# A graph kernel: TensorE gathers 12 groups of edges instead of 7, in a PSUM bank of its own

## What is computed

```python
msgs = z[edge_dst] @ Wd + z[edge_src] @ Ws + edge_weight[:, None] * ww[None, :] + bm
agg = jax.ops.segment_max(msgs, edge_dst, num_segments=n)
hidden = jax.nn.relu(z @ W1a + agg @ W1b + b1);  x1 = layernorm(x + hidden @ W2 + b2)
# then two SAGE convolutions on x1: mean over the edges, two linear maps, relu between
x = layernorm(x1 + conv2(relu(conv1(x1))))
```

## Time and profile before

| | us |
|---|---|
| median of 3 runs | 1136.53 (1135.17 to 1138.17) |
| profiled execution | 1136.4, its span 1134.6 |
| busy: TensorE, VectorE, GpSimd, ScalarE | 997.1, 894.9, 757.0, 500.8 |
| mean granted clock of TensorE | 0.958 |

### The profile page before, as it was taken

The page is one execution under the profiler, slowest core; times in us unless marked ns, Lnnn a source line. Parts: engine busy times, 40 slices in busy tenths (PEclk is TensorE's granted clock), DMA queues, the critical chain, the costliest instruction groups (busy, mean ns, idle before and its releaser), DMA issues.

```text
span 1134.6 us, 23462 instructions
## 1 busy us (share of the span) xinstructions
PE 997.1 (88%) x6407; PEld 735.8 (65%) x6449; DVE 894.9 (79%) x3127; ACT 500.8 (44%) x1434; POOL 757.0 (67%) x802
## 2 busy tenths in 40 slices
PE   4689999999997999978797879886889899899997
PEld 4367767767765777756665656565556577656776
DVE  6488999999886999897777778777788788746455
ACT  3256766666542656533333323333324233312664
POOL 6657777777777777777777777777777777200332
PEclk9789999999997999989898889999999999999999
DMA  8724344344344343334434334433344354446221
GB/s 210 214 61 94 92 98 109 94 99 114 89 97 106 91 119 97 91 85 127 110 87 93 90 97 129 105 91 89 87 132 110 106 150 97 117 134 177 83 58 42
DMA packets 123128, 121.14 MB, mean 107 GB/s; under 512 B 24307, under 2 KB 106392, under 8 KB 122989
## 3 DMA queue, kind: packets, MB, share of 16 engines
q1 hardware_dynamic: 95920, 69.21, 22.7%
q0 software_dynamic: 23968, 49.13, 18.0%
q10 hardware_dynamic: 3101, 1.21, 0.4%
HBM read 105.60 MB, written 13.88 MB: 105 GB/s over the span
## 4 chain that ended last, share of the span: by engine, by line
PE 36%; POOL 30%; issue 15%; DVE 12%; DMA 3%; SPq 2%; ACT 1%; ACTq 1%; DVEq 0%
POOL area L1037 30%; PE bank L1910 7%; PE bank L1748 5%; PE bank L1685 5%; PE bank L1675 3%; PE bank L1626 3%; PE bank L1785 3%; DVE area L1225 2%; DVE area L1209 2%; PE bank L1665 2%; PE bank L1875 2%; DVE area L1208 2%; PE bank L1614 2%; PE bank L1861 1%; PE bank L1706 1%
## 5 line engine op out<-in xcount | busy, mean ns | idle before, releaser
L1037 POOL DMA_INDIRECT area<-zs_d,area x729 | 705.4, 968 | 234.8 <-issue 219.3
L863 ACT CAST adj_w<-bank 128x325 f32 x391 | 176.2, 451 | 472.5 <-PE bank L1685 415.1
L1225 DVE TENSOR_TENSOR_SCAN area<-area,bank 128x512 f32<-128x512 bf16 x196 | 249.7, 1274 | 144.1 <-PE bank L1626 126.5
L1209 DVE TENSOR_SCALAR area<-area 128x325 bf16<-128x325 f16 x782 | 249.5, 319 | 0.0
L1685 PE MATMUL bank<-area 128*128 128x104 f32 x1564 | 234.0, 294 | 0.1
L1208 DVE TENSOR_SCALAR area<-area 128x128 bf16<-128x128 f16 x782 | 212.1, 271 | 0.0
L1685 PEld LDWEIGHTS bank<-area 128*128 128x128 f32 x1564 | 204.7, 204 | 11.3 <-ACT area L869 1.9
L1675 PE MATMUL bank<-area 128*128 128x325 bf16 x782 | 157.2, 316 | 22.0 <-DVE area L1210 15.8
L1626 PE MATMUL bank<-ident,area 128*128 128x128 f32 x734 | 123.1, 291 | 45.8 <-DMA area<-zs_d,area 45.4
L1626 PEld LDWEIGHTS bank<-ident,area 128*128 128x128 f32 x734 | 78.1, 142 | 91.1 <-DMA area<-zs_d,area 57.2
L1748 PE MATMUL bank<-adj_w,area 128*128 128x512 bf16 (+5 forms) x497 | 108.5, 357 | 24.6 <-DMA area<-parts_d 8.6
(11 more groups left out here) (174 smaller groups left out, 1067.6 us busy)
## 6 DMA issues: line engine op xcount, KB each, us to landing
area<-mask_d SPq DMA_DIRECT2D x195, 128.0 KB
area<-zs_d,area POOLq DMA_INDIRECT x729
area<-zs_d SPq DMA_DIRECT2D x640, 0.5 KB
area<-parts_d SPq DMA_DIRECT2D x20, 384.0 KB, 7.6
area<-wp_d SPq DMA_DIRECT2D x195, 9.0 KB
zr_d<-area SPq DMA_DIRECT2D x24, 128.0 KB
area<-zr_d SPq DMA_DIRECT2D x6, 512.0 KB, 4.5
area<-scale_d SPq DMA_DIRECT2D x11, 256.0 KB, 4.3
```

The lines of the kernel that those rows point to most:

```text
L863: nc.scalar.copy(adj[:, :, bass.ds(at, W)], A_BANK[s % 2][:, 0:COLS].rearrange("p (h w) -> p h w", w=W))
L1037: pool.indirect_dma_start(gring[:, g % GR * 4 + s % 2 * 2 + u, :], None, x if g < RAW else zs_d[0:N, :], bass.IndirectOffsetOnAxis(ap=firs ...
L1209: nc.vector.tensor_scalar(hot_d[:, r, u, :], i_key[:, 0:COLS], key_n[:, u, s:s + 1], None, ALU.is_equal)
L1225: nc.vector.tensor_tensor_scan(S[:, g % 2, 0:n], mask[:, g % MR, 0:n], (L_BANK if g in PICKED else T_BANK[g % 2])[:, 0:n], S[:, (g + 1) % ...
```

## The change

- PICKS has 12 groups instead of 7. The first is gathered in slots 20 to 29, and each next one starts in the slot in which the one before is used, up to slot 145. A pick takes 10 or 11 slots, so a slot has two or three one-hots; before, there were 8 to 11 slots, from 7 to 92, with gaps at 48 and 49, 60 to 70, and 80 to 84.
- The picks add up in G_BANK, the bank that was M1. Waits between picks and pieces or degree rows go. Picks now stand in slots with pieces and degree rows.
- x transposed and roots move to M0 (for the last two tiles to G_BANK). New waits: `outputs` of a tile for the roots' copy of the tile before, x transposed for `y_sb`. `roots` and `copy_zr` come one slot sooner.
- `hidden` becomes `hidden_of` on ScalarE, same slot, one activation with bias and relu.
- The one-hots lie in blocks of 128 words, one in each of 2 or 4 rows of the adjacency matrix (SPARE = 1185); the bf16 ones in free columns of aggT, in 3 buffers instead of 4. The group's numbers are made floats in place, and their next load waits for `keyed`.

```diff
-PICKS = ((17, 7), (28, 17), (37, 28), (48, 37), (60, 50), (80, 71), (93, 85))
+PICKS = ((30, 20), (40, 30), (51, 40), (61, 51), (72, 61), (82, 72), (93, 82), (103, 93), (114, 103), (124, 114), (135, 124),
+         (145, 135))
+RAWS = 3
-SPARE = 801
+SPARE = 1185
-        key_i = adj_w[:, spare(0, 512)].bitcast(i32)
-        key_w = adj_w[:, spare(1, 512)]
-        keys = [adj_w[:, spare(2, 256, 256 * i)].bitcast(f16) for i in range(2)]
+        def spare(row, rows):
+            return adj_w.rearrange("p (h n) -> p h n", n=ROW)[:, row:row + rows, SPARE:SPARE + P]
+        key_w = spare(0, 4)
+        key_i = key_w.bitcast(i32)
+        keys = [spare(4 + 2 * i, 2).bitcast(f16) for i in range(2)]
+        hot_b = [aggT[:, FREE + 256 * i:FREE + 256 * i + 256].bitcast(bf16) for i in range(RAWS)]
+        def x_bank(t):
+            return (M0 if t < NT - 2 else G_BANK)[:, P:2 * P]
+        def root_bank(t):
+            return M0[:, P:3 * P] if t < NT - 2 else G_BANK[:, 2 * P:4 * P]
...
                 def load_key(i):
-                        sp.wait_ge(key_float, i)
+                        sp.wait_ge(keyed, i)
...
+                def hidden_of(t):
+                    act.wait_ge(v_ps, t + 1)
+                    nc.scalar.activation(hid(t)[:, 0:k], M0[:, 0:k], ACT.Relu, bias=c0_c).then_inc(hid_sb, 1)
...
                 def make_hot(i, h):
-                    if u >= HOTS:
-                        dve.wait_ge(hot_cast, u - HOTS + 1)
+                    if u >= RAWS:
+                        dve.wait_ge(hot_cast, u - RAWS + 1)
...
                 def x_turned(t):
-                    if t >= 2:
-                        pe.wait_ge(zr_sb, t - 1)
-                    nc.tensor.transpose(M1[:, P:P + k], x_rows(t)[0:k, :], ident[0:k, 0:k]).then_inc(xr_ps, 1)
+                        pe.wait_ge(y_sb, min(t, NT - 2))
+                    if t == NT - 2:
+                        pe.wait_ge(scanned, PICKED[-1] + 1)
+                    nc.tensor.transpose(x_bank(t)[:, 0:k], x_rows(t)[0:k, :], ident[0:k, 0:k]).then_inc(xr_ps, 1)
...
                 def outputs(t):
+                        pe.wait_ge(zr_sb, min(t, NT - 2))
...
                 def half_piece(c, j, h0, h1, at):
-                        pe.wait_ge(scanned, picked_before(PIECES[c][0]) + 1)
...
                 def pick_rows(i, h):
-                        before = len([p for p in PIECES if p[0] < a])
-                        if before:
-                            pe.wait_ge(acc_sb, before)
-                        rows = len([d for d in DEGREE_SLOTS if d < a])
-                        if rows:
-                            pe.wait_ge(deg_sb, rows)
...
-                    for t in tiles(k, 12, -1):
+                    for t in tiles(k, 11):
                         roots(t)
```

More of the change, by code:

```diff
@@ L54 @@
 HOTS = 4
+RAWS = 3
 ROW = AW // 2
-SPARE = 801
+SPARE = 1185
+FREE = 2 * SPARE
 NODES = "a source node, which is below N"
@@ L229, in gnn_kernel @@
         zs_low = [z[:, :, low_at:ROW] for z in zs_r]
-        def spare(row, n, lead=0):
-            return slice(row * ROW + SPARE + lead, row * ROW + SPARE + lead + n)
-        key_i = adj_w[:, spare(0, 512)].bitcast(i32)
-        key_w = adj_w[:, spare(1, 512)]
-        keys = [adj_w[:, spare(2, 256, 256 * i)].bitcast(f16) for i in range(2)]
-        hot_b = [adj_w[:, spare(3 + i // 2, 256, 256 * (i % 2))].bitcast(bf16) for i in range(HOTS)]
-        hot_r = [nc.alloc_sbuf_tensor_at(f"hot_r{i}", [P, 512], f32r, offset=adj_at + 32 * ((ROW * (5 + i) + SPARE) // 8))[:, :]
-                 for i in range(HOTS)]
+        def spare(row, rows):
[3 more added lines that the diff above has]
+        keys = [spare(4 + 2 * i, 2).bitcast(f16) for i in range(2)]
+        hot_r = [nc.alloc_sbuf_tensor_at(f"hot_r{i}", [P, 4 * ROW], f32r, offset=adj_at + 32 * ((ROW * (8 + 4 * i) + SPARE) // 8))[:, :]
+                 .rearrange("p (h n) -> p h n", n=ROW)[:, :, 0:P] for i in range(HOTS)]
         AREA = 15776
@@ L565, in load_key @@
                     if i:
-                        sp.wait_ge(key_float, i)
-                    sp.dma_start(key_i, src[512 * g:512 * g + 512].rearrange("(o e) -> o e", o=1).broadcast_to([P, 512])).then_inc(l_key, 16)
+                        sp.wait_ge(keyed, i)
+                    row = src[512 * g:512 * g + 512].rearrange("(o a e) -> o a e", o=1, e=P)
+                    sp.dma_start(key_i, row.broadcast_to([P, 4, P])).then_inc(l_key, 16)
                 def load_sources():
@@ L885, in copy_x1T @@
                     nc.scalar.copy(zr_of(t)[:, 0, 0:size(t)], M0[:, 384:384 + size(t)]).then_inc(x1T_sb, 1)
+                def hidden_of(t):
+                    k = size(t)
+                    act.wait_ge(v_ps, t + 1)
+                    if 0 < t < NT - 1:
+                        act.wait_ge(x1_st, 32 * t)
+                        act.wait_ge(parts_sb, t)
+                        act.wait_ge(x1T_sb, t)
+                    nc.scalar.activation(hid(t)[:, 0:k], M0[:, 0:k], ACT.Relu, bias=c0_c).then_inc(hid_sb, 1)
                 def copy_zr(t):
@@ L889, in copy_zr @@
                     for a in range(2):
-                        last = nc.scalar.activation(zr_of(t)[:, a, 0:size(t)], M1[:, (2 + a) * P:(2 + a) * P + size(t)], ACT.Identity, bias=b1l_c[:, a:a + 1])
+                        last = nc.scalar.activation(zr_of(t)[:, a, 0:size(t)], root_bank(t)[:, a * P:a * P + size(t)], ACT.Identity, bias=b1l_c[:, a:a + 1])
                     last.then_inc(zr_sb, 1)
@@ L925, in usual @@
                             key_to_float(i)
-                    for t in tiles(k, 13, -1):
+                    for t in tiles(k, 12):
                         copy_zr(t)
@@ L929, in usual @@
                         copy_x1T(t)
+                    for t in tiles(k, 4):
+                        hidden_of(t)
                     for t in tiles(k, 7):
@@ L1249, in scale_from @@
                     nc.vector.reciprocal(row, row).then_inc(scale_sb, 1)
[L1251 to L1258, removed]
                 def stats(t):
@@ L1295, in key_of @@
                     dve.wait_ge(key_float, i + 1)
-                    nc.vector.tensor_scalar(keys[i % 2], key_w, float(CENTER), None, ALU.subtract).then_inc(keyed, 1)
+                    nc.vector.tensor_scalar(keys[i % 2].rearrange("p a (b e) -> p a b e", e=P), key_w.rearrange("p (a b) e -> p a b e", b=2),
+                                            float(CENTER), None, ALU.subtract).then_inc(keyed, 1)
                 def make_hot(i, h):
@@ L1300, in make_hot @@
                     dve.wait_ge(keyed, i + 1)
-                    if u >= HOTS:
-                        dve.wait_ge(hot_cast, u - HOTS + 1)
-                    nc.vector.tensor_scalar(hot_b[u % HOTS], keys[i % 2], node_c[:, h:h + 1], None, ALU.is_equal).then_inc(hot_made, 1)
+                    if u >= RAWS:
+                        dve.wait_ge(hot_cast, u - RAWS + 1)
+                    nc.vector.tensor_scalar(hot_b[u % RAWS].rearrange("p (a e) -> p a e", a=2), keys[i % 2], node_c[:, h:h + 1], None,
+                                            ALU.is_equal).then_inc(hot_made, 1)
                 for k in range(SLOTS):
@@ L1319, in usual @@
                         stats(t)
-                    for t in tiles(k, 4):
-                        hidden(t)
                     if k in DEGREE_SLOTS[:6]:
@@ L1611, in rows_T @@
                 if g in PICKED:
-                    nc.tensor.matmul(L_BANK[:, :], ww9[0:9, :], wp9[:, g % WR, 0:n], start=False, stop=True).then_inc(t_ps, 1)
+                    nc.tensor.matmul(G_BANK[:, :], ww9[0:9, :], wp9[:, g % WR, 0:n], start=False, stop=True).then_inc(t_ps, 1)
                     return
@@ L1741, in roots @@
                     for a in range(2):
-                        last = nc.tensor.matmul(M1[:, (2 + a) * P:(2 + a) * P + k], w1r[:, a * P:(a + 1) * P], zr_of(t)[:, 0, 0:k], start=True, stop=True)
+                        last = nc.tensor.matmul(root_bank(t)[:, a * P:a * P + k], w1r[:, a * P:(a + 1) * P], zr_of(t)[:, 0, 0:k], start=True, stop=True)
                     last.then_inc(zr_ps, 1)
@@ L1784, in pick_rows @@
                     for part_of in (zs_high[at], zs_low[at]):
-                        last = nc.tensor.matmul(L_BANK[:, :], part_of[0:n, h - SPLITS[at][1], :], hot_r[u % HOTS][0:n, :],
+                        last = nc.tensor.matmul(G_BANK.rearrange("p (a e) -> p a e", e=P), part_of[0:n, h - SPLITS[at][1], :], hot_r[u % HOTS][0:n],
                                                 start=h == 0 and part_of is zs_high[at], stop=False)
```

15 lines of the change are left out of this document (4 added, 11 removed).

## The result

The changed kernel takes 1152.39 us, median of 4 runs (1150.39 to 1155.16), beside 1136.3 for the one before. The ratio on record is 1.0126, 95% interval 1.0094 to 1.0157; these two medians alone give 1.0142, inside it. It is slower by 14 to 16 us, where 6.5 were forecast; the sign and the mechanism were right, the size was not. The execution that was profiled is the slowest of the four, 2.8 us above the median.

What follows compares the result with a forecast made beforehand. GpSimd's gathers bound the kernel; alone they would put group 149's gather at 719, but TensorE holds it to 747, against 740.5 before: 1136.4 + 6.5 = 1143 us, own range 1135 to 1152, with rivals 1118 to 1157.

Steps and rivals of the forecast that it cites:

- T: Slots 50 to 146: TensorE's own list of work is longer than GpSimd's, because of where the picks stand.
- the signs of being right: Expected: 709 gathers, 20 to 35 us more GpSimd waiting for TensorE, nearly all in slots 70 to 145.
- GpSimd's part: Main loop: twenty gathers fewer save 25.2 us, 125 more one-hots give back 4.7, leaving 20.5 us.
- rival D: GpSimd's gathers: each new one-hot blocks a gather for its whole length, adding 44.6 us: 1156 us; chance 0.05.
- TensorE's sum: Slots 50 to 146: slots, one-hots, pieces, degree rows and stalls sum to 485.4 us, taken as 476.4.
- the credit: Slots 50 to 146: 9 us off for picks and pieces sharing a slot, bounds 0 and 16.8.
- The three fixed stalls: Slots 66 to 70, 98 to 102, 130 to 134: reciprocal delays store, loads and first piece; 27.6, 24.0, 24.0 us.
- the landmark: First gather of group 149, past the last new pick: from 740.5 to 747.0, so +6.5 us.
- C: Half-piece slots: VectorE is late, half a microsecond in each of 25, giving 1156 us; chance 0.12.
- B: Slots 50 to 146: TensorE absorbs the picks in about 448 us; 1116 us, up to 1130; chance 0.28.
- E: VectorE: the strided one-hots run at 627 ns, 81 us more, giving about 1200 us; chance 0.05.
- The edits costed at nothing: Activation on ScalarE, earlier roots, shared bank M0, key-load wait, three raw buffers, 128-word one-hot rows: priced at 0 us.

Runs made afterwards that it cites:

- high part only: Changed kernel with only each one-hot's product with the table's high part, 300 of 600 matmuls left out: 0.9955 of the kernel before.
- thin pieces: Changed kernel, the eight pieces starting in slots 102 to 138 each keeping one matmul of twelve: 1.0080 of the kernel before, 1144.8 us.
- both reliefs: Changed kernel with only high-part products and every second one-hot a VectorE pass over 16 columns: 0.9890 of the kernel before, 1122.8 us.

## Why the prediction was right in sign and short in size

**What bounds the kernel** was read rightly. GpSimd set the pace before, TensorE and VectorE were within a few per cent of it wherever picks stood; the picks moved into slots that lacked the room, and the ring of four groups carried that back to GpSimd. T is shown from both sides: taking TensorE's work away (high part only, thin pieces) shortens slots 50 to 146 by 25.5 and 20.4 us in the traces, taking the picks out of slots 103 to 145 costs nothing, and eleven picks placed by TensorE's room are faster than the kernel before. One reading of the trace was too strong: behind the wait of 8.57 us GpSimd was held once more, 1.71 us before the gather at 70.88, and only then never again; nothing of the sum hangs on it. Of the signs of being right, the place of the waits came true (45 us of them in slots 70 to 145), their amount did not: 43 us more than before, where 20 to 35 were expected.

**GpSimd's part.** 20.5 us were put on twenty gathers; with both reliefs the trace shows 449.3 us for 448. The price of 0.038 us per one-hot held. GpSimd's gathers after the change, from 270 to 750 us and from 785 to 985, and the one-hots of the first stretch:

```profile
L1051 POOL DMA_INDIRECT area<-zs_d,area x343 | 334.4, 975 | 147.3 <-issue 97.3 <-PE bank L1631 46.1 <-PE bank L1617 4.0
...
L1051 POOL DMA_INDIRECT area<-zs_d,area x159 | 151.7, 954 | 48.5 <-issue 47.9 <-PE bank L1631 0.6
...
L1309 DVE TENSOR_SCALAR area<-adj_w,node_c 128x512 bf16<-128x512 f16 x225 | 70.3, 360 | 0.2
```

A gather is 21 ns longer where one-hots are made: 0.021 x 343 / 225 = 0.032 us per one-hot. This also settles rival D. Its 0.357 us per one-hot would have made these gathers some 230 ns longer. The Trainium skill's page SBUF — State Buffer (section "Who interferes with whom") has VectorE's two-port passes and GpSimd's descriptor writing exclude each other; here, beside two or three one-hot passes in a slot, a gather is those 21 ns longer, and no run shows in which mode the passes run or what each single meeting costs.

**TensorE's sum** was good until its last line. Group 50 opened at 271.3 for 273.5, because GpSimd began group 20 at 121.0 and not 123.0. From there the rows came to 485.4, and 487.4 were measured. The step that failed is the credit: "I take 9", for picks and pieces that share a slot. In the sum it measured nothing. Opening matmuls of groups 111 to 113, and 128 and 129:

```profile
576.12 0.38 PE L1619 MATMUL bank<-area,ww 9*128 9x512 bf16 x1
...
579.98 0.38 PE L1619 MATMUL bank<-area,ww 9*128 9x512 bf16 x1
...
585.14 0.39 PE L1619 MATMUL bank<-area,ww 9*128 9x512 bf16 x1
...
660.87 0.38 PE L1619 MATMUL bank<-area,ww 9*128 9x512 bf16 x1
...
665.80 0.39 PE L1619 MATMUL bank<-area,ww 9*128 9x512 bf16 x1
```

A slot with two one-hots takes 3.86 us, with half a piece too 5.16: 1.30 on top, where half a piece alone was 1.15. A degree slot's share is 1.07 beside one-hots and was 0.93. I read it so, and no run shows it by itself: an otherwise empty slot has small gaps, the first extra work fills them, and the second pays full length. The credit counted the same gaps for the one-hots' sake.

The three fixed stalls took 25.5, 26.1 and 25.9 us for 27.6, 24.0 and 24.0: 77.5 for 75.6. That leaves 409.9 us for the other 84 slots, where the sum without a credit had 409.8. Slot 134 among them took 9.28 us at the lower clock, 3.1 more than slot 102 with the same work (6.15); who counts that with the stall before it finds 3 of the 9, and 5 more in the stalls. The last miss is at the landmark itself: GpSimd was held once more at group 146 and then ran freely, so its gather of 149 came 2.5 us after group 145's matmul and not 1.25. Together: 2.2 sooner at group 50, 9.0 credit, 2.0 in the other terms, 1.7 at the landmark: -2.2 + 9.0 + 2.0 + 1.7 = 10.5, the distance between 747.0 and 757.5. The forecast's own range ended at 1152 with a credit of 0, and 1152.4 was measured. That this fits so well is in part luck: the start at group 50 pays for the 2.0, and the 1.7 at the landmark and the 1.7 behind the loop stand against a median that lies 2.8 below the profiled execution.

**The rivals.** By the time alone C and D, at 1156, lie nearer to 1152.4 than the forecast; the traces decide. B had GpSimd's pace kept; with these twelve picks only a TensorE and a VectorE that are both lighter give nearly that. C, VectorE late by half a microsecond in every piece slot, isn't seen: in slots 112 to 117, all with half a piece, TensorE has no wait above 0.15 us. But VectorE was near, 25 us behind TensorE over slots 50 to 146. E fell with 361 ns.

**The edits costed at nothing** cost 2.5 us together (0.6 to 4.5). Which of them, the runs don't tell; the activation's move isn't seen as a cost.

## What to carry to other kernels

Idle time that a profile shows on an engine is not one sum to spend: add the work up slot by slot over the stretch that the buffers can span, and put the extra where slots are empty; eleven picks so placed gain where twelve evenly spread lose. When three engines run within a few per cent of each other, work moved off the first is worth only the distance to the second (25.5 us here, of 39), and relieving the second alone is worth little (4.6). A credit for overlap that no row shows should be zero in the sum and stand in the range.

## What the runs showed of the hardware

In the changed kernel each of the three fixed stalls was followed by a stretch mostly at TensorE's lower clock (1.2 GHz). Slots 68 and 100 took 8.17 and 8.38 us at granted clocks of 0.62 and 0.60, where slot 140, with the same work, took 5.55: 2.6 and 2.8 us, about as much as the waits before them. The two stretches:

```profile
359.20:367.40 8.20, 8.20 (x38) 6.65 (x38) 5.41 (x22) 4.80 (x13) 3.81 (x4) 0.62 0.42 112
...
519.20:527.60 8.40, 8.39 (x38) 6.85 (x38) 5.22 (x21) 4.79 (x13) 3.77 (x4) 0.60 0.29 79
```

The third shows it best. A wait of 3.79 us for a load at the end of slot 133 was followed by a granted clock of 0.60 from 697 to 705; slot 134 took 9.28 us, and its eight small matmuls took 2.01 us, where those of the next slot took 1.12. Before the change TensorE waited only 1.90 us in that place and kept its clock, slot 134 taking 4.43. The stretch, and those matmuls:

```profile
697.00:705.00 8.00, 8.00 (x33) 6.06 (x33) 3.79 (x14) 2.76 (x7) 3.77 (x4) 0.60 0.40 120
707.00:757.00 50.00, 49.55 (x326) 35.84 (x328) 44.73 (x164) 29.09 (x81) 34.13 (x36) 1.00 0.42 103
```
```profile
699.32 2.01 PE L1690 MATMUL bank<-area 128*128 128x104 f32 x8
...
706.90 1.12 PE L1690 MATMUL bank<-area 128*128 128x104 f32 x8
```

So one late load cost about 3.1 us more than its own length (9.28 for the 6.15 of slot 102), in the execution that was profiled.
